# A graph network's finished blocks on VectorE: one head per instruction instead of all heads at once

## The chip, the cores and the metric

The kernel runs on one core of one Trainium2 chip. The metric is the device time of one execution in microseconds, the median of several runs. Before the change it is 6583.01 us (3 runs, 6576.14 to 6583.16).

## What is computed

A graph of 12500 nodes and 200000 edges, sorted by their target. Two graph attention layers of 4 heads (with a ReLU between), a residual add and a layer norm, then a third attention layer of 8 heads on a linear layer, again with residual and layer norm. Every row has 256 numbers, so a head has C = 64 in the first two layers. Cut to what matters, one attention layer is

```python
h = (x @ W).reshape(n_nodes, H, C)
alpha = leaky_relu(a_src[src] + a_dst[dst])
e = exp(alpha - segment_max(alpha, dst)[dst])
w = e / segment_sum(e, dst)[dst]
out = segment_sum(w[:, :, None] * h[src], dst) + bias
```

In the first two layers each node also has an edge to itself (the self loop). The second layer is followed by

```python
x = layernorm(x + out)
```

## The kernel before, in words

**Phases.** An input phase makes tables and the first product; three edge phases (L = 0, 1, 2, in the text phase 0, 1, 2; `edge_phase`) do one attention layer each; a final phase does the last residual and norm. Nodes are kept in 98 blocks of 128, with sums per block in one large SBUF tensor `acc` (264 columns a block: 256 sums, 4 denominators, 4 maxima, or 256 and 8).

**Windows.** An edge phase walks over 98 windows of 16 tiles of 128 edges. Per window GpSimd gathers the 128 source rows of each tile from the table in HBM (L1032, 16 indirect DMAs, three buffers of rows, so that it may be up to three windows ahead; it waits for TensorE's products of three windows ago). VectorE makes segmented maxima with scans (L1693, L1694 open that work in each window), builds one-hot matrices (L1436), multiplies the rows by their weights (L1444), and TensorE adds them up per block (L1266). VectorE then adds the products to `acc` (L1422). At the head of a window each engine loads words that say where in `acc` the window's blocks lie, into registers (L136); VectorE's extras (the first L1436 of a window, L1498, L1499) stand behind these loads.

**Finished blocks.** In phases 0 and 1 (`CARRY`) a block is finished some windows after its last edge. VectorE does at the end of its window body what `carried` lists, once or once in three windows: `logits` and `shares` (every third window, for three blocks: L1548 to L1554 and L1561 to L1565) make two factors per node and head, `scales[:, 0]` for the gathered sum and `scales[:, 1]` for the node's own row; `value` (every window, one block, L1568 to L1585) puts the block together; `attention` (every third window, L1602 to L1608) splits scores for the lookup of the next phase. Then TensorE turns the block (L1330) and multiplies it with the next weights (L1322), ScalarE copies, and SyncE stores it as table of the next phase.

**`value` before.** It multiplies the block's sum in `acc` by its factor, in place, over all heads (L1571); waits for the node's own row, which SyncE has loaded into `own_row` (`s_loop`); multiplies that by its factor (L1574); adds the two (L1575). In phase 1 (`NORMED`) it waits for the original row, loaded into `turned_x` (`s_res`, SyncE L1089), adds it (L1579), and makes the statistics of the layer norm (L1583, L1585). All are tensor-tensor instructions over 256 columns of fp32 whose factors are broadcast over 64 columns. `link` makes the next instruction of VectorE wait for the semaphore of the one before, since the engine's own order alone does not make a result readable; the number of links of a window is counted ahead (`VALUE_LINKS`). The place of the block in `acc` is a register's value inside the loop; the buffers of `own_row` and `turned_x` alternate and have fixed places.

The order of instructions on each engine is written out by hand; nothing is scheduled. The window body is written out six times for each turn of the loop, behind twelve windows (six in phase 2) written out ahead of it.

Of the kernel before, what the change touches and what calls it, by code (L numbers as in the profile page):

```python
# [28 lines left out]
ALU = mybir.AluOpType  # L29
# [4 lines left out]
P = 128  # L34
# [44 lines left out]
def build_program(nc, t):  # L79
# [3 lines left out]
    def sbuf(stack, name, shape, dtype):  # L83
        return stack.enter_context(nc.sbuf_tensor(name, shape, dtype))
# [35 lines left out]
    def link_on(engine, s, start=0):  # L120

        n = [start]

        def link(ins):
            n[0] += 1
            ins.then_inc(s, 1)
            engine.wait_ge(s, n[0])
        link.n = n
        return link
# [744 lines left out]
    def edge_phase(L):  # L874
        H = HEADS[L]
        C = D // H
# [7 lines left out]
        NORMED = L == 1  # L884
# [5 lines left out]
        with ExitStack() as ph, nc.Block() as block:  # L890
# [14 lines left out]
            if CARRY:  # L905
                own_all = as3
                own_row, turned_x = ([sbuf(ph, f"{tag}{n}{r}", [P, D], F32) for r in range(TURNS)] for n in ("own_row", "turned_x"))
# [5 lines left out]
                scales = sbuf(ph, tag + "scales", [P, 2, BUFS, H], F32)  # L913
# [42 lines left out]
            def pair_of(u, i, n):  # L956

                return i * BUFS + (u - n + 1) // TURNS
# [5 lines left out]
            def place_of(engine, w, n):  # L964

                return w - n if isinstance(w, int) else engine.snap(w - n)
# [41 lines left out]
            def wait_apart(engine, s, n):  # L1008

                if not (isinstance(n, int) and n <= 0):  # L1010
                    engine.wait_ge(s, n)
                    engine.sem_inc(s_apart, 1)

            def count(engine, n):
                return n if isinstance(n, int) else engine.snap(n)
# [399 lines left out]
            def _(dve):  # L1415
# [94 lines left out]
                    message(k, q, n).then_inc(st[f"msg{q}"], 1)  # L1510

                LINKS = (4, 4, 5)
                VALUE_LINKS = 2 if NORMED else 1

                def steps(u, i):

                    turn, k = divmod(u, BUFS)
                    every, earlier = sum(LINKS) + BUFS * VALUE_LINKS, sum(LINKS[:k]) + k * VALUE_LINKS
                    n = [0]
# [12 lines left out]
                def sums_of(first, n):  # L1532

                    sums = acc[:, bass.ds(first * ACC_W, n * ACC_W)] if not isinstance(first, int) else acc[:, first * ACC_W:(first + n) * ACC_W]
                    sums = sums.rearrange("p (b k) -> p b k", k=ACC_W)
                    return sums[:, :, 0:D], sums[:, :, D:D + H], sums[:, :, D + H:MW]
# [30 lines left out]
                def value(link, w, u, i):  # L1567

                    j, r, third, landed = place_of(dve, w, 5), (u - 5) % TURNS, (u - 6) % BUFS, count(dve, pair_of(u, i, 5) * 16)
                    num = sums_of(j, 1)[0].rearrange("p b (h c) -> p (b h) c", h=H)  # L1570
                    nc.vector.tensor_tensor(num, num, scales[:, 0, third, :].unsqueeze(2).to_broadcast([P, H, C]), ALU.mult)  # L1571
                    dve.wait_ge(s_loop[r], landed)
                    out = own_row[r][:].rearrange("p (h c) -> p h c", h=H)
                    link(nc.vector.tensor_tensor(out, out, scales[:, 1, third, :].unsqueeze(2).to_broadcast([P, H, C]), ALU.mult))  # L1574
                    ins = nc.vector.tensor_tensor(out, out, num, ALU.add)  # L1575
                    if NORMED:
                        link(ins)
                        dve.wait_ge(s_res[r], landed)
                        ins = nc.vector.tensor_tensor(own_row[r][:], own_row[r][:], turned_x[r][:], ALU.add)  # L1579
                    ins.then_inc(s["value"], 1)  # L1580
                    if NORMED:
                        wait_apart(dve, s["value"], j)
                        nc.vector.bn_stats(stats[:], own_row[r][:]).then_inc(s["stats"], 1)  # L1583
                        wait_apart(dve, s["stats"], j)
                        nc.vector.bn_aggr(mv[:, r, :], stats[:]).then_inc(s["mean"], 1)  # L1585
# [56 lines left out]
                def carried(w, u, i):  # L1642

                    link, skip = steps(u, i)
                    k = u % BUFS
                    if k == 0:
                        if finished(w, 5):
                            shares(link, place_of(dve, w, 5), in_group(w, 5), count(dve, group_of(u, i, 5)))
                        else:
                            skip(LINKS[0])  # L1650
                    if finished(w, 5):
                        value(link, w, u, i)
                    else:
                        skip(VALUE_LINKS)
                    if k == 1:
                        if finished(w, 9):
                            n = in_group(w, 9)
                            attention(link, place_of(dve, w, 9), n, place_of(dve, w, 7) if n == BUFS else BLOCKS)
                        else:
                            skip(LINKS[1])  # L1660
                    if k == 2:
                        if finished(w, 4):
                            if isinstance(w, int) and w - 4 > BLOCKS - BUFS:
                                dve.wait_ge(s["value"], w - 5)
                                adds(last_offs, W0 + WINDOWS)
                                merge(W0 + WINDOWS)
                            logits(link, place_of(dve, w, 4), in_group(w, 4))
                        else:
                            skip(LINKS[2])
# [121 lines left out]
                link = link_on(dve, s["v1"])  # L1791
# [113 lines left out]
```

## Time and profile before

| | us |
|---|---|
| median of the runs | 6583.01 |
| profiled execution | 6571.58 |
| its span, first to last instruction | 6569.8 |
| VectorE busy | 5272.9 (80%) |
| GpSimd busy | 4601.5 (70%) |
| TensorE busy | 4951.2 (75%) |
| ScalarE busy | 2729.3 (42%) |

The profiled execution is one run; 1.8 us of it lie outside the span. Busy shares are means over stages with different limits. GpSimd's share is lower than its part in the pace, because between two gathers it is not counted as busy. In the names of the views PE is TensorE, DVE VectorE, ACT ScalarE, POOL GpSimd and SP SyncE; a q behind the name is the engine's sequencer, which works on registers and semaphores.

### The profile page before, as it was taken

The page shows a single profiled execution, that of the slowest core. Times are in us where ns is not written, and L with a number is a line of the kernel's source. Part 1 is how long each engine was busy: PE and PEld are TensorE (multiplying, and loading weights), DVE is VectorE, ACT ScalarE, POOL GpSimd, SP SyncE. Part 2 cuts the span into 40 slices and gives each one's busy share as a digit, 9 for nine tenths or more (in the row PEclk, how much of TensorE's full clock was granted, in tenths as well). Part 3 has the DMA queues.
Part 4 walks back from the last instruction along what each step waited for, and adds up shares of the span by engine and source line. Part 5 has one row for each costly group of instructions (what it writes and reads, how often), then busy time and mean ns, then how long its engine had stood idle before and what let it go on. Part 6 is the DMA issues. An engine that isn't in the chain of part 4 may idle for free. (4 is left out here: it accounts for less than half of the span.)

```text
span 6569.8 us, 110146 instructions
## 1 busy us (share of the span) xinstructions
PE 4951.2 (75%) x21652; PEld 3670.2 (56%) x21653; DVE 5272.9 (80%) x16735; ACT 2729.3 (42%) x4351; POOL 4601.5 (70%) x4837
## 2 busy tenths in 40 slices
PE   6787887787878577777777677757777778788776
PEld 5555555555555355555555555535666556566663
DVE  6788888888888688888888888877777777777778
ACT  3333433333333245454454445433333333333335
POOL 2777777777776577676676667637777777777764
PEclk8787877887888678777778778767778777777777
DMA  8555555555554455555555555535555555555545
GB/s 272 149 156 155 156 155 155 158 157 155 155 156 129 122 161 157 155 156 156 152 158 155 153 154 155 155 99 164 161 160 160 160 161 160 162 161 160 161 132 158
DMA packets 505894, 1027.11 MB, mean 156 GB/s; under 512 B 146891, under 2 KB 313199, under 8 KB 504878
## 3 DMA queue, kind: packets, MB, share of 16 engines
q0 software_dynamic: 226208, 633.50, 34.9%
q1 hardware_dynamic: 278798, 382.44, 17.9%
q8 instruction: 477, 7.82, 0.5%
q14 instruction: 411, 3.37, 0.2%
HBM read 931.37 MB, written 84.15 MB: 155 GB/s over the span
## 5 line engine op out<-in xcount | busy, mean ns | idle before, releaser
L1032 POOL DMA_INDIRECT e_rows<-table,loaded x4689 | 4503.7, 960 | 1797.0 <-issue 1377.8
L1266 PE MATMUL e_p_mm<-e_rows,e_onehot 128*128 128x264 f32 x9378 | 2457.4, 415 | 0.0
L1266 PEld LDWEIGHTS e_p_mm<-e_rows,e_onehot 128*128 128x128 f32 x9378 | 1870.0, 207 | 357.4 <-issue 20.2
L1436 DVE TENSOR_TENSOR e_onehot<-e_col,e_p_pair 128x512 f32<-128x512 f32 (+1 forms) x1467 | 948.4, 647 | 659.2 <-issue 619.9
L1444 DVE TENSOR_TENSOR e_rows<-e_rows,e_p_pair 128x1024 f32<-128x1024 f32 x1173 | 1414.0, 1205 | 0.0
L1259 PE MATMUL e_p_mm<-e_xmsg,e_onehot 128*128 128x264 f32 x1764 | 875.4, 668 | 101.9 <-ACT e_p_mm L1133 84.5
L1274 PE MATMUL e_p_one<-ad_parts,e_onehotT 128*128 x5586 | 706.7, 188 | 148.8 <-issue 142.1
L1225 ACT ACTIVATE e_rows<-e_gap 128x64 f32<-128x64 f32 (+1 forms) x294 | 80.5, 274 | 1641.3 <-DVE e_gap L1769 1641.3
L1274 PEld LDWEIGHTS e_p_one<-ad_parts,e_onehotT 128*128 128x128 bf16 x5586 | 549.6, 102 | 329.3 <-issue 189.6
L1139 ACT ACTIVATE e_onehotT<-e_onehotT,minus_pidx 128x2432 bf16<-128x2432 bf16 x294 | 681.1, 2317 | 40.9 <-DMA e_pass<-pass_rows 40.9
L1142 ACT ACTIVATE e_onehotT<-e_onehotT,one_col 128x2432 bf16<-128x2432 bf16 x294 | 682.6, 2322 | 9.6
L1259 PEld LDWEIGHTS e_p_mm<-e_xmsg,e_onehot 128*128 128x128 f32 x1764 | 542.8, 328 | 240.9 <-issue 101.4
L1360 PE MATMUL e_p_small<-ident,e_fwd 64*1 64x64 f32 (+1 forms) x294 | 76.2, 259 | 660.6 <-DVE e_bwd L1694 363.1
L1360 PEld LDWEIGHTS e_p_small<-ident,e_fwd 64*1 64x1 f32 (+1 forms) x294 | 22.7, 77 | 776.2 <-issue 776.2
L1422 DVE TENSOR_TENSOR acc<-acc,e_p_mm 128x264 f32 x1176 | 415.9, 411 | 12.5 <-PE e_p_mm L1266 12.4
L1133 ACT COPY e_p_mm<-iota_d 128x1056 f32<-128x1056 f32 x294 | 304.9, 1037 | 241.9 <-DVEq L1485 240.7
L1693 DVE TENSOR_TENSOR_SCAN e_fwd<-e_mask,e_p_one 64x128 f32<-64x128 bf16 (+1 forms) x294 | 120.4, 410 | 349.0 <-PE e_p_one L1348 348.0
L1498 DVE TENSOR_TENSOR e_xmsg<-e_rows,e_p_pair 128x256 f32 x882 | 358.7, 412 | 0.0
L1348 PE MATMUL e_p_one<-ident,e_srcc 128*64 128x128 f32 (+1 forms) x294 | 84.2, 286 | 285.3 <-ACT e_srcc L1208 119.4
L1232 ACT ACTIVATE e_factor<-e_p_small 128x4 f32<-128x4 f32 (+1 forms) x294 | 51.5, 175 | 550.2 <-PE e_p_small L1384 527.7
L1227 ACT ACTIVATE e_p_pair<-e_gap 128x64 f32<-128x64 f32 (+1 forms) x294 | 72.1, 245 | 496.2 <-DVE e_rows L1444 496.2
L1371 PE MATMUL e_p_small<-ident,e_outf 1*64 1x1 f32 (+1 forms) x294 | 59.2, 201 | 289.1 <-DVE e_outb L1725 287.5
(326 smaller groups left out, 5952.5 us busy)
## 6 DMA issues: line engine op xcount, KB each, us to landing
e_onehotT<-rel_rows SPq DMA_DIRECT2D x294, 608.0 KB
e_rows<-table,loaded POOLq DMA_INDIRECT x4689
e_own_row<-table SPq DMA_DIRECT2D x196, 128.0 KB
table<-e_rows_out SPq DMA_DIRECT2D x98, 132.0 KB
table<-n_rows_out SPq DMA_DIRECT2D x14, 910.0 KB, 17.0
table<-e_rows_out SPq DMA_DIRECT2D x98, 130.0 KB
n_inputs<-in_x_turned SPq DMA_DIRECT2D x14, 896.0 KB, 11.3
e_mask<-mask_rows SPq DMA_DIRECT2D x196, 64.0 KB
```

Source lines behind the costliest of these rows:

```text
L1032: pool.indirect_dma_start(rows[k][:, g, 0:TW], None, table[L], bass.IndirectOffsetOnAxis(ap=idx[k][:, g:g + 1], axis=0)).then_inc(s_gat[k] ...
L1133: nc.scalar.copy(p_mm[:].rearrange("p (r n) -> p r n", n=BANK)[:, :, 0:MW], zero_col.unsqueeze(2).to_broadcast([P, REGIONS, MW])).then_inc ...
L1139: nc.scalar.activation(onehotT[two][:], onehotT[two][:], ACT.Square, bias=minus_pidx[:, 0:1]).then_inc(st["square"], 1)
L1142: nc.scalar.activation(onehotT[two][:], onehotT[two][:], ACT.Relu, bias=one_col[:, 0:1], scale=-1.0).then_inc(st["onehotT"], 1)
L1259: nc.tensor.matmul(p_mm[:, r:r + MW], onehot[:, G + e, :], xmsg[:, e, :], start=False, stop=True, skip_group_check=True)
L1266: ins = nc.tensor.matmul(p_mm[:, bass.ds(region, MW)], onehot[:, g, :], rows[k][:, g, :], start=False, stop=True, skip_group_check=True)
L1274: return nc.tensor.matmul(p_look[:, column], onehotT[k][:, slot * P:(slot + 1) * P], ad_parts[:, bass.ds(ad, 3 * H)], start=False, stop=Tr ...
L1422: last = nc.vector.tensor_tensor(sums, sums, p_mm[:, r * BANK:r * BANK + MW], ALU.add)
L1436: return nc.vector.tensor_tensor(onehot[:, slot:slot + n, :], col[k][:, column:column + n].unsqueeze(2).to_broadcast([P, n, P]), nodes.uns ...
L1444: return nc.vector.tensor_tensor(feats, feats, p_e[:, gs, :].unsqueeze(3).to_broadcast([P, n, H, C]), ALU.mult)
L1498: nc.vector.tensor_tensor(xmsg[:, e, 0:D].rearrange("p (h c) -> p h c", h=H), feats, weight, ALU.mult)
L1693: nc.vector.tensor_tensor_scan(fwd[:], m[0:HG, 0, :], p_src[0:HG, 0:P], -BIG, ALU.add, ALU.max)
```

## The change

`value` is written head by head. A multiply of the own row and the add of the original row become one instruction for each head, which takes the head's factor as a scalar per node; in phase 0, where there is no original row, it is a tensor-scalar multiply. Then, behind one link, a second instruction for each head multiplies the sum in `acc` by its factor and adds the own row to it. The sum in `acc` is only read. The wait for the original row moves ahead of all eight. In phase 0 there is one link, as before; in phase 1 there is one instead of two.

```diff
--- before.py
+++ after.py
@@ -1510,7 +1510,7 @@
                     message(k, q, n).then_inc(st[f"msg{q}"], 1)
 
                 LINKS = (4, 4, 5)
-                VALUE_LINKS = 2 if NORMED else 1
+                VALUE_LINKS = 1
 
                 def steps(u, i):
 
@@ -1568,15 +1568,19 @@
 
                     j, r, third, landed = place_of(dve, w, 5), (u - 5) % TURNS, (u - 6) % BUFS, count(dve, pair_of(u, i, 5) * 16)
                     num = sums_of(j, 1)[0].rearrange("p b (h c) -> p (b h) c", h=H)
-                    nc.vector.tensor_tensor(num, num, scales[:, 0, third, :].unsqueeze(2).to_broadcast([P, H, C]), ALU.mult)
+                    out, kept = (a[r][:].rearrange("p (h c) -> p h c", h=H) for a in (own_row, turned_x))
                     dve.wait_ge(s_loop[r], landed)
-                    out = own_row[r][:].rearrange("p (h c) -> p h c", h=H)
-                    link(nc.vector.tensor_tensor(out, out, scales[:, 1, third, :].unsqueeze(2).to_broadcast([P, H, C]), ALU.mult))
-                    ins = nc.vector.tensor_tensor(out, out, num, ALU.add)
                     if NORMED:
-                        link(ins)
                         dve.wait_ge(s_res[r], landed)
-                        ins = nc.vector.tensor_tensor(own_row[r][:], own_row[r][:], turned_x[r][:], ALU.add)
+                    for h in range(H):
+                        own = scales[:, 1, third, h:h + 1]
+                        if NORMED:
+                            ins = nc.vector.scalar_tensor_tensor(out[:, h, :], out[:, h, :], own, kept[:, h, :], ALU.mult, ALU.add)
+                        else:
+                            ins = nc.vector.tensor_scalar(out[:, h, :], out[:, h, :], own, None, ALU.mult)
+                    link(ins)
+                    for h in range(H):
+                        ins = nc.vector.scalar_tensor_tensor(out[:, h, :], num[:, h, :], scales[:, 0, third, h:h + 1], out[:, h, :], ALU.mult, ALU.add)
                     ins.then_inc(s["value"], 1)
                     if NORMED:
                         wait_apart(dve, s["value"], j)
```

## Rows read from the trace of the kernel before

**Rows 1.** L1693, one a window, in three stretches: start times, waits (us, times)
```profile
L1693 DVE TENSOR_TENSOR_SCAN e_fwd<-e_mask,e_p_one x15: 410/412/414, 159.5 to 435.3; 64x128 f32<-64x128 bf16 x15
...
  PE e_p_one L1348: 32.1, 13
...
L1693 DVE TENSOR_TENSOR_SCAN e_fwd<-e_mask,e_p_one x81: 401/403/413, 455.2 to 2075.2; 64x128 f32<-64x128 bf16 x81
...
  PE e_p_one L1348: 2.2, 5
...
L1693 DVE TENSOR_TENSOR_SCAN e_fwd<-e_mask,e_p_one x79: 401/402/407, 2446.5 to 4173.2; 64x128 f32<-64x128 bf16 x79
```

**Rows 2.** Gathers of GpSimd in phase 0; its waits, phase 0, phase 1
```profile
L1032 POOL DMA_INDIRECT e_rows<-table,loaded x1307: 941/947/1476, 439.2 to 2091.9; - x187
...
  PE e_p_mm L1266: 15.8, 52
...
  PE e_p_mm L1266: 160.2, 130
```

**Rows 3.** Idle of VectorE ahead of L1436, phase 0, phase 1
```profile
  issue: 234.5, 161
...
  issue: 239.8, 150
```

**Rows 4.** Timeline of VectorE in phase 1: start us, us, instruction
```profile
3012.88 0.41 DVE L1571 TENSOR_TENSOR acc<-acc,e_scales 128x256 f32 x1
...
3014.69 0.43 DVE L1583 BATCH_NORM_STATS2 e_stats<-e_own_row 128x6 f32<-128x256 f32 x1 [0.15 <-DVE e_own_row L1579]
...
3015.44 0.19 DVE L1602 CAST ad_parts<-e_scores 128x24 f32 x1
```

**Rows 5.** Timeline of VectorE in phase 0
```profile
1018.68 0.16 DVE L1565 TENSOR_TENSOR e_scales<-e_scales,e_most 128x12 f32<-128x12 f32 x1
1018.98 0.42 DVE L1571 TENSOR_TENSOR acc<-acc,e_scales 128x256 f32 x1
1019.32 0.42 DVE L1574 TENSOR_TENSOR e_own_row<-e_own_row,e_scales 128x256 f32<-128x256 f32 x1
1019.77 0.42 DVE L1575 TENSOR_TENSOR e_own_row<-e_own_row,acc 128x256 f32<-128x256 f32 x1
```

**Rows 6.** The same, 64 columns with a constant
```profile
1015.28 0.21 DVE L1760 SCALAR_TENSOR_TENSOR e_l<-e_l 128x64 f32<-128x64 f32 x1
1015.42 0.14 DVE L1762 TENSOR_TENSOR e_fy<-e_inf,e_adst 1x4 f32<-1x4 f32 x1
...
1015.84 0.19 DVE L1769 TENSOR_SCALAR e_gap<-e_gap 128x64 f32<-128x64 f32 x1
```

**Rows 7.** Timeline at the start: scalar from memory (begin), then constant
```profile
13.60 0.23 DVE L314 TENSOR_SCALAR wrapped<-tile_row,begin 128x13 f32<-128x13 f32 x1
13.73 0.23 DVE L315 TENSOR_SCALAR wrapped<-tile_row,begin 128x13 f32<-128x13 f32 x1
...
15.15 0.17 DVE L319 TENSOR_SCALAR chosen<-tile_row 128x13 f32<-128x13 f32 x1
15.22 0.17 DVE L320 TENSOR_SCALAR lead<-tile_row 128x13 f32<-128x13 f32 x1
```

**Rows 8.** Groups by shape, phase 2: busy us, mean ns; memory scalar, constant
```profile
L1751 DVE SCALAR_TENSOR_TENSOR e_chain_top<-e_p_one,off_row,e_chain_top 1x8 f32<-1x8 f32 x78 | 15.9, 204 | 0.0
...
L1767 DVE SCALAR_TENSOR_TENSOR e_fl<-e_fy 1x8 f32<-1x8 f32 x78 | 11.6, 149 | 0.0
```

**Rows 9.** Register operations (DVEq) of a line; linked step needing one
```profile
L1499 DVEq FUSED_REGOPS  x882: 57/65/71, 168.3 to 6406.9; - x177
...
996.33 0.17 DVE L1549 TENSOR_TENSOR e_scales<-e_most,acc 128x12 f32<-128x12 f32 x1
996.64 0.17 DVE L1550 TENSOR_TENSOR e_scales<-e_scales,e_adst_all 128x12 f32<-128x12 f32 x1
```

**Rows 10.** Waits of the residual add L1579 (us, times)
```profile
  DMA e_turned_x<-in_x_pad: 11.2, 4
```

## The prediction

> **What bounds the kernel now.** I read the views in this order: the pace of the windows in the three edge phases, then who waits in them, then the instructions of the changed step one by one, then the nearest relatives of the new instructions.
>
> The changed step runs in the first two edge phases only, so the first question is what sets their pace. The scan that opens each window starts 81 times from 455.2 to 2075.2 us in phase 0, which is 20.25 us a window; and 79 times from 2446.5 to 4173.2 us in phase 1, 22.14 us a window [rows 1]. GpSimd's gathers explain the first: in phase 0 it issues 1307 gathers in a 1652 us stretch, 1.264 us each, 16 to a window, so 20.2 us, and it waits for TensorE for 15.8 us only. In phase 1 it waits for TensorE for 160.2 us, in 130 places [rows 2]. So phase 0 runs at the gathers' pace and phase 1 does not.
>
> What is late in phase 1 is VectorE. The scan never sat idle in that stretch [rows 1], and VectorE's only long idle spots, ahead of the one-hot of L1436, are put down to issue (239.8 us) and not to another engine: they are its own register loads [rows 3]. VectorE is thus a queue without a wait in it, and each ns put into it counts.
>
> The decisive question is how much room VectorE has in phase 0. There the scan waits for others for 2.2 us in 81 windows; in the first 15 windows, when the finished blocks have not begun or only just, it waits 32.1 us [rows 1]. The issue idle is the same as in phase 1 (234.5 us) [rows 3]. A second way gives much the same: phase 1 has on VectorE what phase 0 has, plus the residual add and the statistics (from 3012.88 to 3015.44 us is 2.56 us, where phase 0 has 1.13 us for the step) [rows 4, 5], 1.43 us, plus the reciprocal and the shift of L1591 and L1593, two short linked instructions like those of rows 9, 0.17 to 0.31 us each. 22.14 less 1.43 and less 0.34 to 0.62 is 20.1 to 20.4 us, an estimate, and phase 0 runs at 20.25. VectorE and the gathers are level there, within about 0.15 us a window.
>
> **The old step.** Phase 0: multiply at 1018.98, multiply at 1019.32, add at 1019.77, behind which the next instruction can follow after 0.34 us, as the second did behind the first: 0.34 + 0.45 + 0.34 = 1.13 us [rows 5]. The second is 0.45 because the add waits for its semaphore. Phase 1: from 3012.88 to the statistics at 3014.69, 1.81 us [rows 4]. Durations of 0.41 and 0.42 us overlap by some 0.07 us, so I count from start to start: 256 columns take 0.34 us, of which about 0.27 us is columns and 0.07 us fixed.
>
> **The new instructions.** None with 64 columns and a scalar read from SBUF exists in the edge phases. A scalar-tensor-tensor of 64 columns with a constant takes 0.21 us and lets its follower start after 0.14 us; a tensor-scalar of 64 columns takes 0.19 us [rows 6], so by the same overlap its follower starts after some 0.11 us. What does a scalar from memory add? Tensor-scalars of 13 columns with one take 0.23 us, those without 0.17 us, and they follow each other at 0.13 instead of 0.07 us [rows 7]. For scalar-tensor-tensors of 8 columns it is 204 ns with against 149 ns without [rows 8]. I take 0.06 us. With 0.21 and 0.19 us as they stand (64 columns are 0.067 us at the pace of the 256, and I count 0.137 and 0.107 to the follower), a scalar-tensor-tensor then costs 0.197 us start to start (0.27 us long) and a tensor-scalar 0.167 us (0.25 us long). The bounds are 0.137 and 0.107 us if the pointer were free, and these values; no row shows more.
>
> **The address.** The sum's place in the accumulator is known in a register only, so each of its four slices needs its own register operation (L1499, with another offset than the line before it, has 882 of its own, 0.065 us each) [rows 9]. The old step had one, ahead of the first multiply, behind long work. Now the first of the four stands behind the link. A linked step that needs such an operation starts 0.14 us behind the end of the one before it (996.33 + 0.17 to 996.64) [rows 9], one that needs none 0.03 us behind (1019.32 + 0.42 to 1019.77) [rows 5], so 0.11 us is added. For the other three I take nothing: 0.065 us is less than the 0.197 us that an instruction takes, and the queue can work ahead of the engine. The bounds are 0 and 0.11 us each.
>
> **Sum for phase 0.** Four tensor-scalars, 3 x 0.167 + 0.25 + 0.03 for the link = 0.78; the address 0.11; four scalar-tensor-tensors 4 x 0.197 = 0.79: 1.68 us against 1.13, so +0.55. One window in three gives back 0.10 us (its first multiply waited for the address at 1018.98, 0.14 us after the end of the share at 1018.84 [rows 5], and the first instruction now has a fixed one), one in three some 0.08 us (the register loads behind the step can start while the short instructions are still queued). That makes +0.50 us. In the first nine windows with a finished block the scan's waits cover it; 83 windows remain: 41 us, less the 2.2 us of waits that are left. I take +39 us, and 2 us for the six blocks behind the last window.
>
> **Sum for phase 1.** Four scalar-tensor-tensors, 3 x 0.197 + 0.27 + 0.03 = 0.89; the address 0.11; 3 x 0.197 = 0.59; the last until the statistics may start 0.27 + 0.15 = 0.42 (that 0.15 us is idle today too [rows 4]): 2.01 us against 1.81, +0.20, less the same 0.10 us in a third of the windows: +0.17. Nothing covers it; 98 blocks: +17 us.
>
> **What moves besides.** The wait for the original rows (turned_x) now stands ahead of the whole step, about 1.2 us earlier, and everything in VectorE's queue stands behind it. Such a wait ended late in 4 of 98 blocks (11.2 us in all) [rows 10]; it can cost 4 x 1.2 us at most, and I take nothing. The product no longer goes back to the accumulator; that frees nothing that anyone waits for. Phase 2 and the rest are untouched.
>
> Together +39 + 2 + 17 = +58 us. The profiled execution took 6571.6 us and would take 6630; it stands 11.4 us below the median of the runs, 6583.0, so the median becomes 6641 us, 0.9% slower.
>
> The Trainium skill (VectorE: DVE Perf Modes, "The TRN2 errata") speaks against the change too: the fixed cost comes once per instruction, so pieces should be of at least 512 elements. With the about 150 cycles at 0.96 GHz that it gives for one operation alone, 0.156 us, and one column a cycle (two for the tensor-scalars), phase 0 would go from 1.27 to 1.65 us and phase 1 from 1.69 to 1.78, an estimate of 83 x 0.38 + 98 x 0.09 = +40 us, 6623 us. The overlapping starts of rows 5 and 6 show half that fixed part, so I keep to the rows.
>
> **Rivals.** (1) A scalar from memory costs nothing in a row of like instructions, because its fetch overlaps the one before. Phase 0: 3 x 0.107 + 0.19 + 0.03 + 0.11 + 4 x 0.137 = 1.20 us, after the give-backs level with 1.13. Phase 1: 3 x 0.137 + 0.24 + 0.11 + 3 x 0.137 + 0.36 = 1.53 us against 1.81, and -0.31 with the give-back: 98 x 0.31 = -30 us, so 6553 us, faster. The sign turns where the price falls under about 0.02 us an instruction (0.06 us makes +58, none makes -30). Against it: consecutive tensor-scalars show the full price in their starts [rows 7]. For it: no scalar-tensor-tensors of this kind follow each other there. Chance 0.09. The Trainium skill (Vector Engine (DVE) Microarchitecture Reference, "Measured stream behaviour on trn2") gives about 75 ns an instruction after queue overlap and names no price for a pointer scalar, which is this case.
>
> (2) The gathers still set phase 0, with 0.2 us or more of room for VectorE that my rows hide in its issue idle. Then phase 0 gives 83 x 0.3 = 25 us or less and the time is 6605 to 6627. That the gathers' pace, 20.2 us, is so close to the windows' 20.25 [rows 1, 2] speaks for it, the 20.1 to 20.4 us for VectorE partly against it. Chance 0.14.
>
> (3) The register operations for three more slices are not hidden: 3 x 0.11 us for 83 and 98 blocks, +60 us, so 6700 us. Only the 0.065 us of rows 9 speak against it, and no row has four of these in a row behind short instructions. Chance 0.12.
>
> (4) Little happens: prices and covers both fall short, within 13 us of 6583. Chance 0.06. That the code does not do what its short description says is true in part: phase 0 has four tensor-scalars among the eight, which is in the sum.
>
> **Numbers.** Forecast, 6627 to 6665 us: 0.59. The range runs from 6598 (rival 2 and some of the lower prices) to 6690 (the part of rival 3 in which about two of the three operations show). About 0.2% is what a measurement of this kernel can tell from no change: faster 0.09, same 0.06, slower 0.85.
>
> **What would show it.** Right: the windows of phase 0 at 20.7 to 20.8 us and of phase 1 at 22.3 us, with phase 2 as before; GpSimd waiting for TensorE in phase 0 as it does in phase 1; scalar-tensor-tensors of 64 columns at 0.26 to 0.28 us, their starts 0.19 to 0.20 us apart, the fifth about 0.14 us behind the end of the fourth. Wrong: starts at 0.13 us (rival 1), phase 0 under 20.6 us with no new waits of GpSimd (rival 2), gaps between the last four (rival 3).

## The result and the profile after

| | before | after |
|---|---|---|
| median of 4 runs, us | 6581.5 (6576.1 to 6583.2) | 6669.8 (6668.8 to 6670.4) |
| profiled execution, us | 6571.6 | 6670.4 |
| span, us | 6569.8 | 6668.5 |

The change makes the kernel slower: the ratio of after to before is 1.0135, interval 1.0118 to 1.0153, or +88 us. The forecast was 6641, range 6598 to 6690. From profile to profile it is +98.8 us, because the profiled execution of before lay 10 us under its median. By stages (from the first scan of one phase to the first scan of the next) the spans differ by +46.6 us in phase 0, +47.1 in phase 1, +0.6 in phase 2 (to its last scan) and +4.4 in the rest. For that rest the profile of before, with 183.4 us, is the shortest of all here; the others at this pace have 185 to 188. (What stands from L1583 on in before stands 4 lines lower in after: the scan is L1697, the statistics are L1587. In after, L1580 in phase 0 and L1578 in phase 1 are the first four instructions of the new step, and L1583 the second four.)

The scan that opens each window, phase 0 then phase 1; the lines answer to [rows 1]. The third field of numbers is the first and last start.

```profile
L1697 DVE TENSOR_TENSOR_SCAN e_fwd<-e_mask,e_p_one x81: 400/405/407, 455.8 to 2121.6; 64x128 f32<-64x128 bf16 x81
...
L1697 DVE TENSOR_TENSOR_SCAN e_fwd<-e_mask,e_p_one x79: 402/405/407, 2493.3 to 4259.9; 64x128 f32<-64x128 bf16 x79
```

(2121.6 - 455.8) / 80 is 20.82 us a window against 20.25 before, and (4259.9 - 2493.3) / 78 is 22.65 against 22.14. The scan has no wait left in phase 0; before it had 2.2 us. Phase 0 was forecast at 20.7 to 20.8 us and came to 20.82. Phase 1 was forecast at 22.3 us and came to 22.65.

The gathers of GpSimd, phase 0 then the waits of phase 1, answer to [rows 2]:

```profile
L1032 POOL DMA_INDIRECT e_rows<-table,loaded x1309: 940/946/1324, 440.0 to 2139.3; - x187
...
  issue: 428.2, 1230
  PE e_p_mm L1266: 28.5, 79
...
  PE e_p_mm L1266: 208.7, 128
```

A gather still takes 0.946 us, but in phase 0 it now comes every (2139.3 - 440.0) / 1308 = 1.299 us instead of 1.264: GpSimd no longer sets the pace; it is held back by the others.

The new step in two windows of phase 0, then in one of phase 1 (start us, us, instruction); these answer to [rows 5] and [rows 4]:

```profile
1034.25 0.79 DVE L1580 TENSOR_SCALAR e_own_row<-e_own_row,e_scales 128x64 f32<-128x64 f32 x4 [0.51 <-DVE e_scales L1565]
1035.18 0.87 DVE L1583 SCALAR_TENSOR_TENSOR e_own_row<-acc,e_scales,e_own_row 128x64 f32<-128x64 f32 x4
...
1053.02 0.79 DVE L1580 TENSOR_SCALAR e_own_row<-e_own_row,e_scales 128x64 f32<-128x64 f32 x4
1054.00 1.10 DVE L1583 SCALAR_TENSOR_TENSOR e_own_row<-acc,e_scales,e_own_row 128x64 f32<-128x64 f32 x4 [0.18 <-DVE e_own_row L1580]
1055.01 0.17 DVE L1606 CAST ad_parts<-e_scores 128x12 f32 x1
...
3001.72 0.85 DVE L1578 SCALAR_TENSOR_TENSOR e_own_row<-e_own_row,e_scales,e_turned_x 128x64 f32<-128x64 f32 x4
3002.72 0.89 DVE L1583 SCALAR_TENSOR_TENSOR e_own_row<-acc,e_scales,e_own_row 128x64 f32<-128x64 f32 x4
3003.76 0.43 DVE L1587 BATCH_NORM_STATS2 e_stats<-e_own_row 128x6 f32<-128x256 f32 x1 [0.15 <-DVE e_own_row L1583]
```

In phase 1 the step takes 3003.76 - 3001.72 = 2.04 us here; before it was 1.81, and 2.01 was forecast. The four of L1578 end at 3002.57, and the first of L1583 starts at 3002.72: the 0.15 us of the link with its address. So the instructions of the step are what they were thought to be, and +0.2 us can't explain the +0.51 us a window.

What can is elsewhere. VectorE's loop goes round once in six windows, between the end of L1554 and the first L1436. Such a passage from the end of the loop's body back to its start is called a turn here. These are one turn of phase 1 before, then one after; DVEq rows are VectorE's sequencer, with the first and last start behind the durations. In both, the branch back is COMPARE_BRANCH, and the four TENSOR_LOADs at L136 open the next window.

```profile
L990 DVEq COMPARE_BRANCH  x1: 56/56/56, 2837.4 to 2837.4; - x1
L990 DVEq FUSED_REGOPS  x1: 104/104/104, 2841.4 to 2841.4; - x1
L136 DVEq ALU_OP  x1: 40/40/40, 2841.5 to 2841.5; - x1
L136 DVEq TENSOR_LOAD <-off_row x4: 315/332/749, 2841.6 to 2843.5; - x4
2843.99 0.55 DVE L1436 TENSOR_TENSOR e_onehot<-e_col,e_p_pair 128x384 f32<-128x384 f32 x1 [6.45 <-issue]
```

```profile
L990 DVEq COMPARE_BRANCH  x1: 56/56/56, 2891.3 to 2891.3; - x1
L990 DVEq FUSED_REGOPS  x1: 104/104/104, 2894.9 to 2894.9; - x1
L136 DVEq ALU_OP  x1: 40/40/40, 2895.0 to 2895.0; - x1
L136 DVEq TENSOR_LOAD <-off_row x4: 316/334/749, 2898.1 to 2899.9; - x4
2900.43 0.55 DVE L1436 TENSOR_TENSOR e_onehot<-e_col,e_p_pair 128x384 f32<-128x384 f32 x1 [8.96 <-issue]
```

Both sequencers stand for 4.0 and 3.6 us behind the branch. Before, the first load follows the ALU_OP at once. After, there is a second stop, from 2895.0 to 2898.1. Over the 13 turns of phase 1 the passage from the start of VectorE's last instruction (L1554) to the first L1436 takes 6.27 us on average before and 8.55 after. The same passage between two windows inside the loop's body takes 2.2 to 2.6 us on average in both. In phase 0 the turns take 5.78 and 5.91 us, in phase 2 5.34 and 5.22. 13 x (8.55 - 6.27) = 30 us. The sum of VectorE's idle ahead of L1436 in phase 1, 239.8 us in [rows 3], shows the same 30 us:

```profile
  issue: 272.1, 151
```

What ends these stops shows in the DMA traffic, where some queues are of the kind "instruction". While VectorE stands for the first time (2891.3 to 2894.9) and for the second (2895.0 to 2898.1), the queue list of after (packets, MB, share of 16 engines) has one packet each on q14:

```profile
q14 instruction: 1, 0.01, 0.5%
...
q14 instruction: 1, 0.01, 0.6%
```

Each is of 8192 bytes. They start at 2893.0 and 2896.3, and VectorE goes on 1.9 and 1.8 us behind their starts. In all 40 turns of the three phases, before and after alike, a q14 packet starts 1.0 to 2.3 us behind the branch and the next instruction follows 1.8 us behind that in most turns, 2.4 at most; a second packet starts 3.4 to 5.2 us behind the branch. Only in phase 1 of after does an instruction wait for the second. My reading is that VectorE's instructions are being fetched, and that the place of the loop in the program decides whether one fetch shows or two. The times alone do not prove that; experiments 1, 2 and 8 test it.

### The profile page after: what moved, and what is told of

Same layout as the page of the kernel before. It is cut to its first block and busy times, and to the rows that moved or that the text cites. A ratio compares the mean times of both kernels' runs of the same rounds, so it can differ in the third digit from the quotient of the medians.

```text
span 6668.5 us, 111467 instructions
## 1 busy us (share of the span) xinstructions
PE 4950.7 (74%) x21652; PEld 3674.8 (55%) x21653; DVE 5326.7 (80%) x17617; ACT 2727.3 (41%) x4351; POOL 4578.0 (69%) x4837
## 5 line engine op out<-in xcount | busy, mean ns | idle before, releaser
L1436 DVE TENSOR_TENSOR e_onehot<-e_col,e_p_pair 128x512 f32<-128x512 f32 (+1 forms) x1467 | 949.0, 647 | 689.0 <-issue 644.6
L1697 DVE TENSOR_TENSOR_SCAN e_fwd<-e_mask,e_p_one 64x128 f32<-64x128 bf16 (+1 forms) x294 | 120.7, 410 | 344.7 <-PE e_p_one L1348 343.7
```

What stands on the lines that cost most here:

```text
L1436: return nc.vector.tensor_tensor(onehot[:, slot:slot + n, :], col[k][:, column:column + n].unsqueeze(2).to_broadcast([P, n, P]), nodes.uns ...
L1697: nc.vector.tensor_tensor_scan(fwd[:], m[0:HG, 0, :], p_src[0:HG, 0:P], -BIG, ALU.add, ALU.max)
```

## Experiments

**A chip of another pace.** The first four kernels ran on a chip on which the kernel before takes 9639.6 us (31 runs). They were the kernels of experiments 1 to 4 below. They took 9660.2 us (six empty instructions, on after; ratio 1.0020, 0.9999 to 1.0041), 9655.3 (148 of them, on before; 1.0018), 9655.1 (change in phase 0 alone; 1.0011) and 9649.9 (in phase 1 alone; 1.0008), where 6603 to 6638 us had been expected. The profile page of the first shows why they tell little:

```profile
L1032 POOL DMA_INDIRECT e_rows<-table,loaded x4689 | 4443.9, 948 | 4946.2 <-PE e_p_mm L1266 2524.0
```

A gather is issued in the usual 0.948 us, but the idle time ahead of gathers is 4946 us instead of 1797 (before), 2524 of it waiting for TensorE, and a window takes 30 to 33 us. There VectorE has 8 us to spare in each window, and the times of the four tell little about its work. The turns of VectorE's loop are as on the other chips, though: 6.38 us and 8.43 us in phase 1 for the first two. I ran all four again, on chips of the ordinary pace. All numbers of experiments 1 to 4 are from those.

**1. Move the loop, keep the change.** Six increments of a semaphore that nothing waits for stand ahead of the windows of phase 1 on VectorE. They do nothing but move what follows by six instructions:

```diff
+                if NORMED:
+                    for _ in range(6):
+                        dve.sem_inc(s_apart, 1)
                 walk(dve, body)
```

> The kernel of after_shift6 once more, on another chip: on the first one both this kernel and the kernel before took 9640 to 9660 us, with GpSimd waiting over 1000 us a phase for the gathered rows' use, so that VectorE's time hardly showed, while the turn of phase 1's loop did fall to 6.4 us. Where the kernel before takes about 6580 us, the theory (place in the program) gives 6670 - 32 = 6638 us, the rival (nothing but GpSimd's and VectorE's own work counts) 6670.

Measured: 6644.7 us (6642.0 to 6648.4), ratio to before 1.0097 (1.0080 to 1.0114): 25 us less than after, with six instructions more. The turn takes 6.17 us on average instead of 8.55, and the second stop is gone:

```profile
L136 DVEq ALU_OP  x1: 40/40/40, 2890.5 to 2890.5; - x1
L136 DVEq TENSOR_LOAD <-off_row x4: 315/332/749, 2890.6 to 2892.4; - x4
...
2892.95 0.56 DVE L1436 TENSOR_TENSOR e_onehot<-e_col,e_p_pair 128x384 f32<-128x384 f32 x1 [5.82 <-issue]
...
L1697 DVE TENSOR_TENSOR_SCAN e_fwd<-e_mask,e_p_one x79: 402/405/405, 2493.2 to 4232.9; 64x128 f32<-64x128 bf16 x79
```

The windows of phase 1 go to 1739.7 / 78 = 22.30 us. That is +0.17 us on before, as was forecast for the step.

**2. Move the loop, without the change.** In the kernel before, 148 such increments bring the loop to where after has it:

```diff
+                if NORMED:
+                    for _ in range(148):
+                        dve.sem_inc(s_apart, 1)
                 walk(dve, body)
```

> The kernel of before_shift148 once more, on another chip. The turn of phase 1's loop took 8.4 us there, as the theory (place) has it; where the kernel before takes about 6580 us this should now show in the time: 6580 + 30 + 4 = 6614 us. Rival (the longer turn is made up for elsewhere): 6584 us.

Measured: 6606.2 us (6604.6 to 6612.2), ratio 1.0043 (1.0026 to 1.0060), +26.6 us against 6579.6 for before. The turn takes 8.67 us, and the scan's pace is (4175.6 - 2453.7) / 77 = 22.36 us over the stretch shown, and 22.42 over the 78 windows over which before has 22.14:

```profile
L136 DVEq ALU_OP  x1: 40/40/40, 2852.0 to 2852.0; - x1
L136 DVEq TENSOR_LOAD <-off_row x4: 315/333/748, 2854.4 to 2856.2; - x4
...
2856.73 0.56 DVE L1436 TENSOR_TENSOR e_onehot<-e_col,e_p_pair 128x384 f32<-128x384 f32 x1 [8.21 <-issue]
...
L1693 DVE TENSOR_TENSOR_SCAN e_fwd<-e_mask,e_p_one x78: 403/405/406, 2453.7 to 4175.6; 64x128 f32<-64x128 bf16 x78
```

Not all of the +26.6 us is the place. The 148 increments themselves take VectorE 14.0 us:

```profile
L1811 DVEq EVENT_SEMAPHORE  x148: 21/21/21, 2208.2 to 2222.2; - x148
```

The first scan of phase 1 is 14.2 us later than before (2222.7 against 2208.5), the thirteenth 7.2 us (2453.7 against 2446.5). The first windows have waits and make up half (24.0 us of waits ahead of their scans before, 16.6 here), and 6 to 7 us stay. That leaves some 20 us for the place; the 78 windows give 78 x 0.28 = 22 us. Of the 13 x 2.40 = 31 us by which the turns are longer, 9 to 11 us do not show in the time.

The two experiments show the cause from both sides: the place gives 25 us when it is left and costs 20 to 22 when it is taken up, with the old step as with the new one.

**3. The change in phase 0 alone.** The new step stands behind the `if`, the old one behind the `else`:

```diff
+                    if not NORMED:
...
+                    else:
...
```

> The new step in phase 0 alone, once more on another chip. Its loops begin at other places than 4098 in VectorE's program and its turns took 5.3 and 6.3 us. Theory: 20.81 us a window in phase 0, 22.14 in phase 1, 81 x 0.57 = 46 us, 6626 us where the kernel before takes 6580. Rival (the gathers cover half of it): 6603 us.

Measured: 6623.3 us (6620.8 to 6629.2), ratio 1.0067 (1.0050 to 1.0084), +43.7 us. The scans of phase 0 and phase 1:

```profile
L1708 DVE TENSOR_TENSOR_SCAN e_fwd<-e_mask,e_p_one x82: 402/405/406, 455.4 to 2139.2; 64x128 f32<-64x128 bf16 x82
...
L1708 DVE TENSOR_TENSOR_SCAN e_fwd<-e_mask,e_p_one x78: 401/405/406, 2490.0 to 4193.8; 64x128 f32<-64x128 bf16 x78
```

The first line gives 1683.8 / 81 = 20.79 us a window where 20.7 to 20.8 were forecast. For this part 41 us in all were forecast, and 43.7 came. If the gathers had still set the pace (rival 2) it would have been 25 us or less.

**4. The change in phase 1 alone** (the same edit with `if NORMED`).

> The new step in phase 1 alone, once more, where the kernel before takes about 6580 us. Its phase 1 loop begins at instruction 3974 and its turn took 6.2 us on the first chip. Theory (place): only the instructions' own cost is left, about 0.2 us a window; the kernel shifted by six minus the one with the step in phase 0 alone is 6645 - 6623 = 21 us, so 6580 + 21 = 6601 us. Rival (the body's length costs it): 6580 + 50 = 6630 us.

Measured: 6591.3 us (10 runs, 6587.2 to 6595.9), ratio 1.0017 (1.0007 to 1.0026), +11.3 us; 17 was forecast. Here the loop lies elsewhere and its turns take 6.09 us. The step takes 2.04 us, +0.22 on before, but the window only +0.10: small stops at other lines are shorter or gone. Together, experiments 3 and 4 give 55 us where experiment 1 has 65. These 10 us stay open; the profile of experiment 1 has 4.9 us more than before in phase 2, where nothing was changed, and phase 0, the same in both, is 3.7 us longer in it than in experiment 3.

**5. The pointer's price.** All factors of the new step are replaced by the constant 0.5, so the kernel leaves the true factors out. The places in the program are those of after.

```diff
-                        own = scales[:, 1, third, h:h + 1]
+                        own = 0.5
...
-    ins = nc.vector.scalar_tensor_tensor(out[:, h, :], num[:, h, :], scales[:, 0, third, h:h + 1], out[:, h, :], ...)
+    ins = nc.vector.scalar_tensor_tensor(out[:, h, :], num[:, h, :], 0.5, out[:, h, :], ...)
```

> The changed kernel with the constant 0.5 for both factors, so that none of the eight instructions reads a scalar from memory (the factors are thus left out of the result). Theory (a scalar from memory costs about 0.06 us an instruction, also among its like): scalar-tensor-tensors of 64 columns start 0.13 to 0.14 us apart instead of 0.196, tensor-scalars 0.10 to 0.11 instead of 0.163, and the first instruction behind the link stands as far behind the end of the fourth as in the changed kernel, 0.15 us. On a chip on which VectorE sets the pace that takes away 8 x 0.06 = 0.5 us a window in phases 0 and 1. Rival (the price is that of three operands or of short instructions, not of the scalar): the starts stay at 0.19 us or more.

Measured, one run: 6608.6 us, before 6579.9. Four instructions of each kind, in phase 0 and in phase 1:

```profile
1042.32 0.48 DVE L1580 TENSOR_SCALAR e_own_row<-e_own_row 128x64 f32<-128x64 f32 x4
...
3012.13 0.63 DVE L1578 SCALAR_TENSOR_TENSOR e_own_row<-e_own_row,e_turned_x 128x64 f32<-128x64 f32 x4 [0.20 <-DVE e_scales L1565]
3012.89 0.63 DVE L1583 SCALAR_TENSOR_TENSOR e_own_row<-acc,e_own_row 128x64 f32<-128x64 f32 x4
```

0.63 us where after has 0.85 to 0.89, and 0.48 where it has 0.79. From start to start (medians) a scalar-tensor-tensor takes 0.136 us instead of 0.196 and a tensor-scalar 0.102 instead of 0.163. The pointer (the factor read from memory) costs 0.060 and 0.061 us an instruction: what [rows 7] show for 13 columns holds for 64. Rival 1 falls. Its time, 6553 us, would not have been reached with free pointers either: this kernel is 28.7 us above before. By stages, phase 0 is 18.6 us longer than before and phase 1 9.1 us: its turns of 8.33 us lengthen phase 1, and a step of 1.62 us against 1.82 shortens it. (Phase 2, where nothing was changed, is 7.7 us longer in this one profile too, so a few us are uncertain.)

The Trainium skill (Vector Engine (DVE) Microarchitecture Reference, "Measured stream behaviour on trn2") gives one column in 1.04 ns and about 75 ns an instruction: 64 columns make 0.142 us, an estimate. The row with a constant agrees within 0.006 us; the price of a pointer is what it does not have.

**6. The address.** The sum is read from block 1 in every window, so the kernel leaves the other blocks' sums out, and no register is needed for its place.

```diff
-                    num = sums_of(j, 1)[0].rearrange("p b (h c) -> p (b h) c", h=H)
+                    num = sums_of(1, 1)[0].rearrange("p b (h c) -> p (b h) c", h=H)
```

> The changed kernel with the sum read from a fixed block of acc (block 1, so the result is another), which takes the four register operations a window away, and with them 45 instructions of VectorE's program. Theory (address behind the link): the first instruction behind the link starts 0.03 to 0.04 us behind the end of the fourth instead of 0.15, 0.11 us less a window in both phases, 2 x 98 x 0.11 = 22 us, and the loop of phase 1 begins at 4075, where no stop stood so far, 30 us: 6669 - 22 - 30 = 6617 us. Rival 3 of the prediction (the other three operations cost too): 0.3 us a window more, under 6570 us.

Measured: 6609.7 us (6604.6 to 6610.7), ratio 1.0046 (1.0029 to 1.0063).

```profile
2991.37 0.85 DVE L1578 SCALAR_TENSOR_TENSOR e_own_row<-e_own_row,e_scales,e_turned_x 128x64 f32<-128x64 f32 x4
2992.26 0.87 DVE L1583 SCALAR_TENSOR_TENSOR e_own_row<-acc,e_scales,e_own_row 128x64 f32<-128x64 f32 x4
```

2991.37 + 0.85 = 2992.22, and the next starts at 2992.26. In phase 1, 0.035 us lie behind the link in the median instead of 0.149: the address costs 0.11 us there, as was read from [rows 5, 9]. The four of L1583 take 0.87 us in the median with a fixed address and with four register operations alike: the other three operations cost nothing that shows, and rival 3 falls. The whole is 35 us under experiment 1; 0.11 us in 181 windows is 20 us of that, and I have not traced the rest.

**7. The turn itself.** In the kernel before, VectorE's loop goes round once in twelve windows:

```diff
-                with engine.Fori(unrolled, WINDOWS // UNROLL) as i:
-                    for u in range(UNROLL):
-                        at(i * UNROLL + u, u, i)
+                with engine.Fori(unrolled // turns, WINDOWS // UNROLL // turns) as j:
+                    for part in range(turns):
+                        i = j * turns + part
+                        for u in range(UNROLL):
+                            at(i * UNROLL + u, u, i)
...
-                walk(dve, body)
+                walk(dve, body, unrolled=2, turns=2)
```

(Phase 2 then has twelve windows ahead of its loop instead of six.)

> The kernel before, but VectorE's loop has twelve windows written out instead of six, in all three phases, so that it turns 7 times in a phase instead of 14 (15 in phase 2). A turn costs 5.5 to 6.3 us where the same step inside the body takes 2.3, so 3.2 us in phase 0 and 4.0 in phase 1. Theory (the turn is VectorE's own time, and phase 1 is VectorE's): 7 x 4.0 = 28 us less in phase 1; phases 0 and 2 run at the gathers' pace of 20.2 us and gain at most a few us; 6580 - 28 = 6552 us. Rival (the turn's wait is for other engines or hidden): no change, 6580.

Measured: 6540.1 us (6538.0 to 6542.3), ratio 0.9940 (0.9923 to 0.9956), 39 us less than before.

```profile
L1695 DVE TENSOR_TENSOR_SCAN e_fwd<-e_mask,e_p_one x79: 402/405/407, 2442.1 to 4136.5; 64x128 f32<-64x128 bf16 x79
```

21.72 us a window in phase 1 against 22.14. One turn in twelve windows is saved. At 6.27 us less some 2.4 us of a passage inside the body, that makes 3.9 / 12 = 0.32 of these 0.42 us. The turns that are left take 5.78 us, which makes another 0.5 / 12 = 0.04.

**8. No loop on VectorE at all.** In the kernel before, all 98 windows of each phase are written out for VectorE; its program has 34271 instructions instead of 7283.

```diff
-                walk(dve, body)
+                walk(dve, body, unrolled=WINDOWS // UNROLL)
```

> The kernel before with no loop on VectorE at all: all 98 windows of each phase are written out. The twelve-window loop took 39.5 us off, where seven turns less make 28 us in phase 1. Theory (turns are VectorE's own time, and registers become constants): seven more turns of 4.0 us go in phase 1, and about 0.1 us a window for register operations behind links; 6540 - 28 - 10 = 6502 us. Rival (a program four times as long has to be fetched all the time, and stops at the ends of its pieces come instead): 6540 us or more.

Measured: 6477.2 us (6474.4 to 6477.9), ratio 0.9844 (0.9828 to 0.9861): 103 us less than before and 193 less than after. The scans of phase 0 and phase 1:

```profile
L1694 DVE TENSOR_TENSOR_SCAN e_fwd<-e_mask,e_p_one x80: 403/412/414, 454.2 to 2046.8; 64x128 f32<-64x128 bf16 x80
...
L1694 DVE TENSOR_TENSOR_SCAN e_fwd<-e_mask,e_p_one x79: 402/405/414, 2458.8 to 4099.9; 64x128 f32<-64x128 bf16 x79
```

Phase 1 runs at 21.04 us a window (-1.10), phase 0 at 20.16 (-0.09), because the gathers bound it. The passage to the first L1436 takes 2.0 to 2.3 us on average, whichever window it is. For six windows that is 13.0 us; before it is 6.27 for the one with the turn and 12.3 for the five others. So 5.6 us are saved in six windows, 0.94 of the 1.10 us. Not all of this is the fetch: the places of the blocks are constants here, and VectorE's sequencer has 12 register operations a window where before has 28. The instruction packets of q14 over the whole execution, before, then experiment 7, then this one:

```profile
q14 instruction: 411, 3.37, 0.2%
...
q14 instruction: 361, 2.95, 0.1%
...
q14 instruction: 299, 2.45, 0.1%
```

The program written out takes fewer packets, not more, and none of the stops of a turn is left. The rival that was recorded, a program that stops for its fetches all the time and takes 6540 us or more, falls.

## Why the prediction was right, and where it was not

**Who is late.** Right. Phase 0 passed from the gathers' pace to VectorE's, phase 1 stayed with it, phase 2 did not move (20.26 and 20.28 us). VectorE had at most the 0.15 us of room in phase 0 that was estimated: experiment 3 gives +43.7 us where 41 was forecast, and rival 2 (25 us or less) falls.

**The new instructions and the address.** Right within 0.02 us, in the median: 0.196 and 0.163 us start to start (0.197 and 0.167 forecast), 0.149 us behind the link in phase 1 and 0.160 in phase 0 (0.14), 0.060 us for a pointer (0.06).

**The size in phase 0.** The sum came out by errors that cancel. A window grew by 0.57 us, from 20.27 to 20.84 over 78 windows. In two windows of three the step takes 1.79 us on average where 1.68 was forecast, +0.67 us on before: small stops such as the one at 1054.00 above, where four instructions take 1.10 us instead of 0.87, were not in the sum. In the third window, where the register loads follow, the time to the next instruction grew by 0.45 us only: the give-back forecast there as 0.08 us is 0.22. The other give-back, 0.10 us at the first instruction of the step, came in one such window of two (0.29 us behind the start of L1565 before, 0.20 after); in the other, always the same body of the loop, it is 0.67 us, the row at 1034.25. That is +0.05 us a window. Elsewhere 0.03 us was added (behind L1554) and some 0.1 us went at other lines, of which the waits of the scan, 0.02 us a window, are the only ones for another engine. So VectorE had next to no room in phase 0; that the total is near the forecast is in part luck.

**Phase 1.** This is the step that failed, as a sum that was not complete: "Nothing covers it; 98 blocks: +17 us". +0.17 us a window is what the edit costs where the turns stay as they were (experiment 1: 22.30 against 22.14), but the phase became 47 us longer. The measured time lies inside the range, but the mechanism that brought it to the upper part is none of those that the range was made of. The sum counted what is between the instructions of a step and not where they lie. The new step has more instructions, and it is written out many times: counted in the programs, 3950 of VectorE's instructions stand ahead of the loop of phase 1 before and 4098 after. 13 turns at 2.28 us more are 30 us, and experiments 1 and 2 measured 25 and 20 to 22.

The warning was in [rows 3]. I read the issue idle ahead of L1436 as "its own register loads"; of the 239.8 us in phase 1 some 80 lie in 13 turns of 6.1 us each, where four loads take 2 us (2841.6 to 2843.8 above). The timeline of one turn would have shown it.

The Trainium skill (Runtime: NRT & Kernel Launch, "Instruction fetch mechanics") has the rule that I left out. An engine holds two blocks of its program, the next one is fetched while the present one runs, and a branch to a place that is not held must wait for a fetch. The trace agrees: each turn stands 2.8 to 4.2 us behind its branch, until 1.8 to 2.4 us after the start of an instruction packet. The rule gives also the second stop, if the target stands at the end of a block: of 256 instructions by the page, 4096 is the 16th boundary, and in my count, which begins at 0, the instruction that waits is number 4100. The loops of phase 1 in these kernels fit: with 3950, 3974, 4074, 4075 and 4104 instructions ahead of them they have turns of 6.0 to 6.4 us, and with 4098 (in three kernels) 8.3 to 8.7. The loop of phase 2 in after has 6018 ahead of it, two short of another multiple of 128 in the same count, and no second stop, which speaks for 256. The twelve-window loop of experiment 7 has 4717 ahead of it and turns of 5.8 us. Not settled is that the packets have 8192 bytes each, half of what the page gives a block, and where the four come from by which my count is off. Nor could the second stop be forecast from the page without that count. As a rival it would have been worth naming; with the price known now, 30 us more than the forecast would be 6671.

**What the record asked to see.** Starts 0.19 to 0.20 us apart: there. The fifth about 0.14 us behind the end of the fourth: there, 0.15. GpSimd waiting in phase 0 as in phase 1: only in part, 28.5 us beside TensorE's name (15.8 before) and 428.2 under issue (383.8 before), against 208.7 beside TensorE in phase 1.

**The sum as measured.** Phase 0 43.7 us, phase 1 11.3, the place 20 to 25: 75 to 80 of 88 us. 8 to 13 us stay open. Part may be the small stops described at the end, which lie elsewhere in each kernel; that is argued, not shown.

## What to carry to other kernels

An instruction cut in pieces pays its fixed part and its pointer again in each piece: here 0.07 and 0.06 us a piece, which is why eight pieces of 64 columns lost to three and four instructions of 256 although they made fewer passes over the data. Before an edit on a busy engine is priced, look at the turns of its loop as well: an edit anywhere ahead moves them, and a comparison of two variants can differ by their places alone, so a few empty instructions ahead of the loop are a cheap control. If one engine sets the pace and has a loop, try to write the loop out or make its turns rarer for that engine alone: here that gave 103 and 39 us, more than anything else tried.

## What was not expected of the hardware

A turn of VectorE's loop costs 3 to 4.5 us beyond what the same passage costs inside the body, in every phase and at every turn, and 5.7 to 7 us in phase 1 of after, though the same instructions have run one turn before.

There are small stops in straight code too. In phase 1 of after, in one of the six window bodies, the first L1583 starts 0.797 us behind the start of the last L1578 in 13 of 13 passes, elsewhere 0.40 to 0.44. In phase 0 one L1583 starts 0.414 us behind the one before it in 13 of 13, elsewhere 0.196. Behind each of these 26 stops a q14 packet starts 0.6 to 1.5 us later, so I take them for the moments at which the sequencer asks for its next piece; that is argued, not shown. The instruction that waits in phase 1 is number 4360, four behind 4100 + 256, but in phase 0 it is 1755, which is at no such distance. The stops cost 0.22 to 0.39 us each. The Trainium skill (Runtime: NRT & Kernel Launch, "Instruction fetch mechanics") calls the crossing from one block to the next mostly hidden; if these stops are crossings, it is not hidden among short instructions.

One chip of those used needs 9640 us for a kernel that takes 6580 on the others, at the same gather instructions; what is slow there was not looked for.
